# Routed experts beside sparse attention: token rows gathered ahead of the routed addition, their weights copied out first, second buffers for the last four attention groups, another order of loads and vector steps

## What is computed

```python
xn = _layernorm(x)
x = x + attn0(xn) + moe(xn)         # block 0
xn = _layernorm(x)
x = x + attn1(xn) + ffn1(xn)        # block 1

# attn0: 128 heads, keys are scalars; 32 largest and 32 smallest keys of each head
k_idx = jnp.argsort(keys, axis=-1)
attn_top = softmax(q[..., None] * top_keys[:, :, None, :])   # the same for bottom
out = q_pos * out_top + (1.0 - q_pos) * out_bot              # then @ Wo.T

# moe: 64 experts, top 6 of each token, capacity of 128 tokens for one expert
xe = xpad[buf]                                               # (64, 128, 256) gathered rows
h = silu(xe @ w1.T) * (xe @ w3.T);  ye = h @ w2.T
routed = sum over the 6 chosen of ye[fe, pc] * gate
z = silu(xf @ sw1.T) * (xf @ sw3.T) @ sw2.T                  # shared expert
```

## Time and profile before

| | |
|---|---|
| Time, three runs | 618.04, 605.39, 614.75 us; median 614.75 |
| The profiled execution's own time | 613.87 us |
| Its span, first to last instruction | 612.1 us |
| Busy, share of the span | PE 76%, DVE 62%, POOL 39%, ACT 31% |
| Mean granted TensorE clock | 0.883 |
| DMA | 91.80 MB, 150 GB/s over the span |

### The profile page before, as it was taken

How to read it: one execution, slowest core, us unless ns; L and a number is a source line. 1 busy time by engine, 2 the same in 40 slices (tenths; PEclk the granted TensorE clock), 3 DMA queues, 4 the chain that set the end, 5 groups by cost and what they waited for, 6 DMA issues and landing times.

```text
span 612.1 us, 9668 instructions
## 1 busy us (share of the span) xinstructions
PE 465.3 (76%) x2928; PEld 302.7 (49%) x2928; DVE 381.4 (62%) x1067; ACT 187.7 (31%) x479; POOL 237.6 (39%) x210
## 2 busy tenths in 40 slices
PE   4922999888777898778688978536889988657766
PEld 2611555455445554545455545213634777545645
DVE  4897687844553655455536556425769868577984
ACT  2651322223332333233333332211265303021122
POOL 3153466556555555555455542000002053022444
PEclk9965999979988977899789887857889999798898
DMA  8921498879878787877787874440000277566502
GB/s 313 341 84 43 109 297 186 206 176 238 211 197 203 173 196 201 212 184 197 197 201 167 211 163 84 120 172 14 2 0 1 52 182 104 112 121 126 129 7 70
DMA packets 63422, 91.80 MB, mean 150 GB/s; under 512 B 21120, under 2 KB 42464, under 8 KB 63264
## 3 DMA queue, kind: packets, MB, share of 16 engines
q1 hardware_dynamic: 50496, 70.19, 42.0%
q0 software_dynamic: 12896, 21.24, 17.6%
HBM read 72.89 MB, written 18.51 MB: 149 GB/s over the span
## 4 chain that ended last, share of the span: by engine, by line
PE 28%; DMA 28%; DVE 14%; SPq 11%; issue 9%; POOL 5%; ACT 4%; DVEq 0%; ACTq 0%; POOLq 0%
PE ps L1418 20%; DMA big<-kr_dram 9%; DMA big<-k_img 8%; DMA big<-tok_tab,big 7%; SPq L485 6%; POOL routed L624 2%; DMA big<-idx_dram 2%; PE ps L1423 2%; DVE big L1096 2%; PE ps L1521 2%; SPq L567 2%; DVE big L1011 1%; POOL big L617 1%; DVE big L1009 1%; DVE big L1396 1%
## 5 line engine op out<-in xcount | busy, mean ns | idle before, releaser
L1418 PE MATMUL ps<-big 128*128 128x352 f32 (+4 forms) x768 | 241.9, 459 | 9.2 <-DVE big L1074 6.2
L1418 PEld LDWEIGHTS ps<-big 128*128 128x128 f32 (+2 forms) x768 | 149.9, 208 | 71.4 <-issue 29.9
L624 POOL DMA_INDIRECT routed<-big x64 | 101.9, 1592 | 130.4 <-ACT big L792 114.4
L617 POOL DMA_INDIRECT big<-tok_tab,big x64 | 63.3, 990 | 31.2 <-issue 30.9
L1074 DVE COPY big<-ps 88x256 f32<-88x256 f32 x64 | 26.7, 417 | 66.3 <-PE ps L1506 64.3
L1066 DVE SCALAR_TENSOR_TENSOR big<-big,ps 128x176 f32<-128x176 f32 x64 | 21.6, 337 | 65.6 <-ACT big L787 65.5
L1423 PE MATMUL ps<-cst,big 128*128 128x128 f32 x144 | 32.5, 311 | 36.9 <-DMA big<-tok_tab,big 34.2
L782 ACT ACTIVATE big<-ps 128x256 f32<-128x256 f32 x64 | 24.6, 384 | 107.3 <-PE ps L1423 107.2
L1418 PE MATMUL ps<-xnT,big 128*128 128x512 f32 (+1 forms) x104 | 50.1, 623 | 0.9 <-ACT xnT L723 0.9
L787 ACT ACTIVATE big<-ps 128x176 f32<-128x176 f32 x64 | 20.3, 318 | 96.5 <-PE ps L1418 96.5
L805 ACT ACTIVATE big<-ps 128x512 f32<-128x512 f32 x64 | 34.7, 595 | 45.9 <-PE ps L1521 45.7
(11 more groups left out here) (187 smaller groups left out, 668.0 us busy)
## 6 DMA issues: line engine op xcount, KB each, us to landing
big<-in_w SPq DMA_DIRECT2D x64, 352.0 KB
big<-in_w SPq DMA_DIRECT2D x64, 176.0 KB
big<-q_dram SPq DMA_DIRECT2D x64, 72.0 KB
big<-kr_dram SPq DMA_DIRECT2D x24, 192.0 KB
big<-kr_dram SPq DMA_DIRECT2D x72, 64.0 KB
big<-idx_dram SPq DMA_DIRECT2D x16, 256.0 KB, 7.4
kr_dram<-big SPq DMA_DIRECT2D x12, 256.0 KB, 4.5
routed<-big POOLq DMA_DIRECT2D x2, 1152.0 KB, 16.0
```

Source lines behind the costliest of these rows:

```text
L617: nc.gpsimd.indirect_dma_start(xe[:, e % SLOTS, :], None, tok_tab, bass.IndirectOffsetOnAxis(ap=sidx[:, e:e + 1], axis=0))\
L624: nc.gpsimd.indirect_dma_start(routed[e % 2], bass.IndirectOffsetOnAxis(ap=sidx[:, e:e + 1], axis=0), ye[:, e % 2, :], None, compute_op=AL ...
L1418: last = nc.tensor.matmul(o, w, m, start=(n == 0), stop=(n == len(pairs) - 1))
```

## The change

1. **POOL.** The gather of expert e+5 is put ahead of routed_add(e) (one extra gather stands before the loop), and a gather waits for a new semaphore `s_xefree` in place of y.
2. **ACT.** After the copy of the transposed tokens, ACT copies the expert's column of gate weights (128x1) into `gate[:, u]` and signals `s_xefree`; the scaling reads `gate`.
3. **Second buffers** `skgs[1]`, `qxs[1]`, `idxbs[1]` lie over early buffers (`sc`, `sr`, `skey`, part of them `absd`) and are used for groups 13 and 15, with semaphores of their own. SP issues all loads of group 13 right behind its loop.
4. **SP's order.** In the loop the queries and keys come before the weights for slot 1, and the positions before those for slot 2. Behind the loop: group 13, queries 12, positions 14, queries 14, the routed sums, queries 15, positions 15, `w5`.
5. **DVE's order.** Key search, one-hot rows, place_values, normalise and ternary are split and moved, in part ahead of `hidden(e+1)`. The ternary blocks of both weight tensors are done in quads 1 to 8, two in a quad; none is left behind the loop.
6. **PE and ACT in the last four groups.** The values of group n+1 come behind x1_product; before, they stood between the logits. ACT copies oT ahead of the values.

```diff
+            sp.wait_ge(s_abs, 2)
+            second = IN_LOOP + 1
             with sp.Fori(1, IN_LOOP) as n:
                 for u in range(SLOTS):
                     next_weights(n + LAG, u, bass.ds(n + LAG, 1))
-                    if u == 1:
+                    if u == 0:
                         sp.wait_ge(s_lp, n * 4)
                         q_and_keys(bass.ds(n, 1))
-                    if u == 2:
+                    if u == 1:
                         sp.wait_ge(s_hot, n * 4 + 4)
                         positions(bass.ds(n + 1, 1))
-            for n in range(IN_LOOP, NG):
-                sp.wait_ge(s_lp, 4 * n)
-                q_and_keys(only(n))
-                if n == NG - 2:
...
+            q_and_keys(only(second), qxs[1], skgs[1], s_qxl2)
+            positions(only(second), idxbs[1], s_idx2)
+            sp.wait_ge(s_lp, 4 * IN_LOOP)
+            q_and_keys(only(IN_LOOP))
+            sp.wait_ge(s_hot, 4 * IN_LOOP + 4)
+            positions(only(IN_LOOP + 2))
+            sp.wait_ge(s_lp, 4 * IN_LOOP + 4)
+            q_and_keys(only(IN_LOOP + 2))
+            for i in range(2):
+                sp.wait_ge(s_sc[i], 16 * (1 + E // 2))
...
+            sp.wait_ge(s_lp, 4 * IN_LOOP + 8)
+            q_and_keys(only(IN_LOOP + 3), qxs[1], skgs[1], s_qxl2)
+            sp.wait_ge(s_hot, 4 * IN_LOOP + 8)
+            positions(only(IN_LOOP + 3), idxbs[1], s_idx2)
+            sp.wait_ge(s_y, E + 1)
+            sp.dma_start(w5, w_rkvgo).then_inc(s_w5, 16)
...
             def token_gather(e):
                 if e >= SLOTS:
-                    pool.wait_ge(s_y, e - SLOTS + 2)
+                    pool.wait_ge(s_xefree, e - SLOTS + 1)
...
+            token_gather(SLOTS)
             for e in range(E):
+                if e + SLOTS + 1 < E:
+                    token_gather(e + SLOTS + 1)
                 routed_add(e)
-                if e + SLOTS < E:
-                    token_gather(e + SLOTS)
...
-            def tokens_in(e, u):
+            def tokens_in(e, u, group):
+
                 act.wait_ge(s_xeTp, e + 1)
                 nc.scalar.activation(xeT[:, u % 2, :, :], PS[0][:, 0:D].rearrange("p (c n) -> p c n", c=DC),
                                      ACT.Copy).then_inc(s_xeT, 1)
+                nc.scalar.activation(gate[:, u:u + 1], gates[:, u, u, group], ACT.Copy).then_inc(s_xefree, 1)
...
             for n in range(IN_LOOP, NG):
                 exps(n, range(4))
-                if n + 1 < NG:
-                    values_out(n + 1)
                 if n == IN_LOOP:
                     act.wait_ge(s_qst, 64)
                 oT_copy(n - IN_LOOP)
+                if n + 1 < NG:
+                    values_out(n + 1)
...
             for e in range(LAG * SLOTS):
                 u = e % SLOTS
+                r = e // 2 + 1
                 hidden_T(e, u)
-                hidden(e + 1, (u + 1) % SLOTS)
...
+                if e % 2 == 0:
+                    if r < 8:
+                        largest(r, 0)
+                        largest(r, 1)
+                    hidden(e + 1, (u + 1) % SLOTS)
+                    if r < 8:
+                        where(r, 0)
+                else:
+                    if r < 8:
+                        where(r, 1)
+                        remove(r, 0)
+                    hidden(e + 1, (u + 1) % SLOTS)
...
                     hidden_T(e, u)
+                    if u == 0:
+                        place_values(n)
+                        one_hot(n + 1, 0)
+                    if u == 1:
+                        one_hot(n + 1, 3)
+                        if done:
+                            normalise(*done, slice(0, 5))
                     if u == 2:
                         out_copy(n)
+                    if blocks and u == 3:
+                        ternary(0, *blocks)
                     if not last or u + 1 < SLOTS:
                         hidden(e + 1, u + 1)
                     if u == 0:
-                        place_values(n)
-                    if u < 2:
-                        one_hot(n + 1, 2 * u)
-                        one_hot(n + 1, 2 * u + 1)
-                    if done and u == 0:
-                        normalise(*done, slice(0, 5))
+                        one_hot(n + 1, 1)
+                        one_hot(n + 1, 2)
                     if done and u == 1:
                         normalise(*done, slice(5, NORM))
-                    if done and u == 3:
-                        ternary(*done)
+                    if blocks and u == 2:
+                        ternary(1, blocks[0] - 1, blocks[1])
...
                 for c in range(4):
-                    logits(n, c)
-                    if c % 2 and n + 1 < NG:
-                        if c == 1:
-                            pe.wait_ge(s_vraw, n + 1)
-                        values(n + 1, c // 2, slice(n + 1, n + 2))
+                    logits(n, c, t % 2 == 1)
                 oT_transposes(t)
                 weighted(n)
                 if t == 0:
                     pe.wait_ge(s_wo0, 48)
+                    pe.wait_ge(s_hs, NPAIR)
                 x1_product(t)
+                if n + 1 < NG:
+                    pe.wait_ge(s_vraw, n + 1)
+                    for side in range(2):
+                        values(n + 1, side, slice(n + 1, n + 2))
                 to_natural(n)
```

More of the change, by code:

```diff
@@ L835, in _, with quad @@
                     values_out(0)
-                tokens_in(e + 2, u)
-                scale_out(e, u, g * 32 + 16 * (1 + u // 2), gates[:, u, u, g:g + 1])
-            def quad(n, group, last=False):
+                tokens_in(e + 2, (u + 2) % 4, slice((e + 2) // 4, (e + 2) // 4 + 1))
+                act.wait_ge(s_xefree, e + 1)
+                scale_out(e, u, g * 32 + 16 * (1 + u // 2))
+            def quad(n, group, after, last=False):
                 for u in range(SLOTS):
@@ L848, in quad @@
                     if not last or u + 2 < SLOTS:
[L849 to L850 removed]
+                        tokens_in(e + 2, (u + 2) % 4, group if u < 2 else after)
+                    act.wait_ge(s_xefree, e + 1)
+                    scale_out(e, u, n * 32 + (LAG * 32 + 16 * (1 + u // 2)))
             with act.Fori(0, IN_LOOP - 1) as n:
[L853 to L854 removed]
+                quad(n, bass.ds(n + LAG, 1), bass.ds(n + (LAG + 1), 1))
+            quad(IN_LOOP - 1, slice(QUADS - 1, QUADS), None, last=True)
             for n in range(IN_LOOP, NG):
                 exps(n, range(4))
[L857 to L858 removed]
                 if n == IN_LOOP:
@@ L1054, in remove @@
                   .then_inc(s_dk, 1)
-            select(0)
-            remove(0)
+            for step in (largest, where, remove):
+                for side in range(2):
+                    step(0, side)
             dve.wait_ge(s_absp, 1)
@@ L1095, in one_hot @@
                         dve.wait_ge(s_valp, n)
[L1096 removed]
+                nc.vector.tensor_scalar(hot[:, k, :], idxbs[second], const("vpos")[:, k:k + 1], None, ALU.is_equal)\
                   .then_inc(s_hot, 1)
@@ L1178, in _, with quad @@
                     one_hot(0, 2 * u + 1)
-            def quad(n, done=None, last=False):
+            def quad(n, done=None, blocks=None, last=False):
                 for u in range(SLOTS):
@@ L1514, in down, with logits @@
                     .then_inc(s_yp, 1)
-            def logits(n, c):
+            def logits(n, c, second=False):
+                skg, qx = skgs[second], qxs[second]
                 if c == 0:
-                    pe.wait_ge(s_qxl, n * 80 + 80)
+                    if second:
+                        pe.wait_ge(s_qxl2, 80 * (1 + (n - IN_LOOP) // 2))
+                    elif isinstance(n, int) and n > IN_LOOP:
+                        pe.wait_ge(s_qxl, 80 * (IN_LOOP + 2))
+                    else:
+                        pe.wait_ge(s_qxl, n * 80 + 80)
                 if c >= 2:
```

101 lines of the change are left out of this document (52 added, 49 removed).

## The result

The changed kernel takes 561.15 us (median of four runs, 556.6 to 564.07), the kernel before 612.75 (605.39 to 618.04); the ratio is 0.922, 95% interval 0.910 to 0.935. The forecast was 548 us with a range of 526 to 578. The profiled execution took 564.07 us, its span is 562.3 us, 49.8 less than before.

The account below looks back on a forecast made before the run. PE's waits for token rows and keys, and the lower clock after them, were taken to bound the kernel. Savings 7.5 + 43.3 + 16 + 0.5 = 67.3 us off 614.75 gave 547.5, say 548 us; range 526 to 578.

Parts of the forecast that it names:

- the gather wait: PE's wait for token rows in a quad, 1.46 us in the middle one; forecast to go with earlier gathers.
- the key wait: PE's wait for keys at a quad's seam, 1.03 us in the middle quad; forecast to go with earlier loads.
- the quad: Loop of quads: each of eleven full quads was to take 16.3 us, saving 41.3 us in all.
- with no wait at the seam there is no reason for the lower clock: Quads: PE was to stay at full clock, as in the first quad, which showed 1.00.
- The twelfth quad: Last quad, without further gathers: was to lose its two waits and half a clock stretch, 2 us.
- The first 16 experts: Stage of the first 16 experts: waits of 4.4 us and 3 us of low clock go, 7.5 us saved.
- The last four groups: Groups 12 to 15: waits for one-hot rows and keys go, less what is given back, 16 us saved.
- The 64 weight copies: Gate weight copies on ACT: taken as 0 cost; 12 us at 0.19 each if their cover fails.
- the additions' loop: Floor of a quad from scaling, issuing and landing routed additions: 13.0 us, 15 if landings take 6.6.
- The moved steps: DVE steps in the quads: fit beside `up` and tanh; up to 0.6 us per quad come back.
- The waits come back at the seam: Rival: transfers slow, PE idles and the clock falls once per quad, 18.0 us quads, 569 us; chance 0.23.
- Slower by late positions: Rival: late positions delay DVE's one-hot rows and `hidden`; slower from quads of 22.1 us on; chance 0.02.

Follow-up runs that it names:

- run 1: The kernel before with only the gathers ahead and the gate weights copied out; 600.38 us, ratio 0.989.
- run 2: The kernel before with only the new order of queries, keys and positions in SP's loop; 607.5 us, ratio 0.999.
- run 9: The kernel before with the gathers ahead and SP's new loop order together, old DVE order and old last groups; 566.8 us, ratio 0.944.
- run 7: The changed kernel with half of each w_13 load left out from the second quad of experts on; 547.31 us, ratio 0.895.
- run 6: The changed kernel with four tables for the routed additions and four ye buffers in place of two; 562.23 us, ratio 0.916.
- run 8: The changed kernel with each slot's w_13 load asked for one slot earlier, same bytes; 561.58 us, ratio 0.918.
- run 10: The kernel before with half of each w_13 load left out from the second quad of experts on; 599.7 us, no clear ratio.
- run 12: The changed kernel with the routed sums last and group 13's loads behind the queries of group 12; 562.47 us, ratio 0.934.
- run 3: The kernel before with only the second buffers, the load order behind the loop and the moved values in the last four groups; 596.45 us, ratio 0.982.
- run 11: The changed kernel with the routed sums loaded behind the queries and positions of group 15; 562.49 us, ratio 0.932.
- run 4: The kernel before with only DVE's new order and the ternary blocks all in quads 1 to 8; 607.37 us, ratio 0.989.

## Why the prediction was right, and where a term was off

**The mechanism** held. The two waits at the seam went, the clock came back with them, and the DMA rate was late next. Runs 1, 2 and 9 show more than was argued: I worked out the gather wait and the key wait one by one, and they are one obstacle, of which either part alone gives 2 to 3 us and both 33.6. The clock came back in most quads, not in all.

**The mis-sized term is the quad.** I took 16.3 us, "between PE's floor and the DMA at the share that the first quad held", and the eleven quads took 17.3 in the mean: 190.7 against 179.3 us, 11.4 too many. Most of that is one step of the prediction, "with no wait at the seam there is no reason for the lower clock". The eight quads at full clock took 16.6 us, 2.6 us over the forecast in all eight together; the three in which the clock fell took 8.9 us more than forecast. A wait at the seam had stayed in the second (1.72 us for keys, 0.70 for weights); the fourth idles 1.74 us ahead of an `up`, and the ninth 1.0, 1.0 and 1.4 us. The rest is the DMA share. I worked 16.2 us out of a share of 1.0; the changed kernel held 0.91, and 17.34 x 0.91 = 15.8 us of the engines' time is close to the 16.2 of the sum, divided by a share that no quad reached (0.98 at most). 0.95 was the row for a whole quad, and it gave 17.1 in the prediction's own text; the 1.09 over 5 us was a peak and no rate. Run 9 shows that a clock of 1.00 isn't enough either: 17.0 us per quad at a share of 0.89.

Run 7 shows that bytes shorten the quad, runs 6 and 8 that it wasn't one particular wait. Whether the bytes count as a rate or because every transfer lands sooner isn't told apart: the same 7.9 MB took 10.1 us off the kernel before too, at a share of only 0.81 (run 10).

Of the 67.3 us that the forecast adds up, the spans show 49.8. The 17.5 missing are these 11.4, 4.3 of the twelfth quad and 3.3 of the start, less 1.4 that the last groups gave beyond theirs.

**The twelfth quad** was to lose 2 us and gained 2.3. The working counted only what it was rid of. The group 13 loads (0.6 MB) were added to it, though run 12 speaks against them as the cause. PE idles in it for 3.4 us, before for 1.1; 1.48 of them are for weights, and 1.36 for ACT's scaling, which waits for additions to land. Every kernel with that part shows 16.7 to 18.6 us, every one without it 14.9 to 15.9.

**The first 16 experts:** 7.5 us forecast, 7.5 measured, which is luck. With the odd start of the profile before taken in, the first logits come 4.2 us earlier. Runs 3 and 10, which leave this stage as it was, took 77.0 and 75.3 us for it, and the kernels with all of the change 71.1 to 73.6 (75.05 in run 6, with its early start).

**The last four groups:** 16 forecast, 17.4 measured. The positions of group 15 are late as forecast, but not for the reason given: DVE waits 5.5 us for them, of which PE feels 2.2 us and another 1.3 behind it (3 forecast), and run 11 shows that the sums ahead of them aren't what makes them late.

**The 64 weight copies** were put at nothing, with 0.19 us each as their size. From the changed kernel, 133 to 322 us, grouped by line:

```profile
L804 ACT ACTIVATE gate<-big 128x1 f32 x43 | 8.4, 194 | 0.0
```

0.19 us it is. Run 1, which has them, is not slower than before.

**Additions and weights.** I had put the additions' loop at 13.0 us per quad, and 15 with late landings; ACT did wait for landings, 14.0 us, but taking that wait away (run 6) gave nothing. "The weights for slot 1 have a whole quad to land" was wrong: `up` of slot 1 stands in slot 0 of the next quad, so they had some 8 us, and they are the weights that PE waits for at 271.65. It didn't matter for the time (run 8).

**DVE.** The moved steps were to fit beside `up` and cost up to 0.6 us per quad. Alone they took 9.7 us off the quads in the one profile of run 4; beside the pair they show no gain, and perhaps a cost of 3 to 5 us over eleven quads (run 9). Why they help the kernel before, through the clock or through hidden stalls, stays open.

**The rivals.** "The waits come back at the seam" has a part in it: 17.3 us lies between its 18.0 and the forecast's 16.3, and the second, fourth and ninth quad fell to 0.73, 0.91 and 0.91 in clock. Most of the quads' missing time lies in these three. "Slower by late positions" shows as 7.7 us of DVE waits, far below the point from which it decides. The Trainium skill's 358 GB/s ("DMA: Bandwidth & Descriptors", Specifications), which I set aside, would have made the transfers hidden. It is stated there as a limit and not as a rate for transfers of this kind; single slices of the pages, all at the start of the program, reach it or pass it (354 GB/s in the changed kernel, 411 in run 6). As a rate to plan with it fails for this kernel, whose quads ran at 230 GB/s with a share of 0.91 and got 15.4 us shorter by 7.9 MB less.

## What to carry to other kernels

Waits that end at the same point of a loop can be one obstacle: here the edits that each remove one of them gave 2 to 3 us alone and 33.6 together, so try them as a pair before dropping either. When a loop gets faster, divide its DMA time by the share that whole iterations hold (0.9 here), not by 1, and look at iterations one by one: three of eleven with a fallen clock held most of the missing time. When every transfer makes somebody wait a little, moving one of them ahead may only change who waits, as in runs 6 and 8; then count bytes.

## What was unexpected

The part of the program that the change leaves nearly alone (it moves one ternary block and the `w5` load) varies more than the small effects under study. From the first logits of group 15 to the end the profiles took 195.0 us before and in the changed kernel (612.1 - 417.12, 562.3 - 367.35), 184.1 in run 9 (564.0 - 379.92) and 187.1 in run 4 (593.0 - 405.91). Run 9 has the very code of the kernel before there. So a total of one kernel can be 5 to 10 us off for reasons that lie elsewhere, and runs 4 and 9 are better read by their windows. A kernel with runs 3 and 9 in one, without DVE's new order, is what the table points to as the next to try; it wasn't run.
